# Layer 3's expert weights: from one DMA per part to one load and VectorE copies into a ring

## The chip, the cores and the metric

One NeuronCore of a Trainium2 chip runs the whole program; nothing is split over cores. The metric is the device time of one execution in microseconds. The kernel before takes 620.84 us, the median of 3 runs (620.84 to 621.14).

## The reference

Four layers run one after the other on x of 4 x 256 x 256 (1024 tokens of 256 channels). In each layer a bidirectional decay recurrence over the tokens gives weights by which sigmoid(x) is multiplied, and a mixture-of-experts FFN of that product is added to x:

```
x = x + L0_ffn(L0_cond(x, ...), ...)   # 48 kept experts, top 8, capacity 96
x = x + L1_ffn(L1_cond(x, ...), ...)   # 8 experts of 176, top 2, and a shared one
x = x + L2_ffn(L2_cond(x, ...), ...)   # 14 experts of 176, top 2, and a shared one
x = x + L3_ffn(L3_cond(x, ...), ...)   # 16 experts of 128, top 2, weights unpacked from integers
```

The change is in layer 3's FFN, where per token t and expert e:

```
logits = log_sigmoid(x @ gate_weight.T); probs = softmax(logits); topw, topi = top_k(probs, 2)
w_up, w_down = (q - 8) * blocks_scale * global_scale        # 16 x 256 x 128, 16 x 128 x 256
a = square(relu(x @ w_up[e]));  y = sum over e of (a * wdense[t, e]) @ w_down[e]
```

## The kernel before, in words

The engines run their own instruction streams and meet at semaphores. For layers 1 to 3 the 2048 pairs of a token and its expert are sorted by expert into blocks of 128 rows. In layer 3 a block has two parts of 64 rows, each with an expert of its own, since few tokens go to each of 16 experts: 24 blocks (`BK[3]`), 48 parts. The two parts are two column tiles of TensorE. VectorE computes in `block_experts` (L1306) a table `be`, which says for every part which expert it belongs to.

What happens to block b of layer 3:

- GpSimd (POOL) gathers its 128 token rows from `ctab` in DRAM into one of six buffers `xs` (`gather2`, L1682), about five blocks ahead.
- TensorE transposes them (`block_turn`, L707), ScalarE moves them to `xT_s` (`block_move`, L924), TensorE multiplies with the up weights of the two parts (`block_up`, L733, 8 matmuls), ScalarE takes the relu (`block_act`, L932), VectorE squares it (`block_hidden`, L1346), TensorE transposes that (`turn_h`, L748), ScalarE moves it (`move_h`, L939), TensorE multiplies with the down weights (`block_down`, L765, 4 matmuls), ScalarE moves the result to `o_s`, one of three buffers (`block_out`, L946), and POOL scatters it to `ybuf` in DRAM (`scatter2`, L1689).

The order of the instructions is written out by hand. TensorE's loop (L845) is, in iteration b: turn block b+2, up of block b+1, transpose of the hidden of block b, down of block b-1. POOL's loop is gather b+5, scatter b-1, and VectorE's has `block_hidden(b)` alone in layer 3.

The weights: layers 1 and 2 unpack the 16 experts of layer 3 beside their own work and store them in DRAM (`w3`: per expert 128 rows of 512 numbers, 256 up columns and 256 down columns, 256 KB). `load_parts` (L417) on SyncE's (SP's) queue then copies for every part its expert from `w3` to one of 16 places `w3r` in `wR`: a register is loaded from `be` (L425) and a DMA issued with it (L426); TensorE waits for each place (L729), and from part 16 on a DMA waits until the down product of an old part is done. `wR` holds layer 2's up weights until that layer's last block.

After the blocks SP reads `ybuf` back into `ysb` in two DMAs of 1 MB (L473), ScalarE and VectorE weigh the two rows of each token (L954, L1352), TensorE turns them back (`final`, L781), VectorE adds them to x (L1216), and x is stored.

Of the kernel before, what the change touches and what calls it, by code (L numbers as in the profile page):

```python
# [5 lines left out]
P = 128  # L6
# [43 lines left out]
NG = P // GROUP  # L50
SHW = [P, P, SH1 - 2 * P]
NSH, SHEAD = 6, 3
XB, OB, WB = 6, 3, 16

RW = 2 * KT * E2 * I2
UP1 = RW - 2 * KT * E1 * I1
assert E1 * 2 * C <= UP1 and WB * 2 * C <= RW
BM, GM = max(BK), max(k * n for k, n in zip(NP, BK))  # L60
RL = [0, UNITS, 2 * UNITS, E2 * 2]
assert RL[3] >= 3 * UNITS
# [39 lines left out]
def build(nc, xT, fT, cond, wu, o2n_row, o2n_col, gwT, rconst, gscale, wglu, wq, s_up, s_down, sel3,  # L102
          ident, tri, iota, out):
    with ExitStack() as ctx:
# [3 lines left out]
        def sem(name):  # L108
            return ctx.enter_context(nc.semaphore(name))
# [95 lines left out]
        with ExitStack() as tables:  # L205
            def sbt(name, shape, dt=F32):
# [28 lines left out]
        half_t = sb("half_t", [P, BM])  # L235
        idx_g = sb("idx_g", [P, BM], I32)
        idx_s = sb("idx_s", [P, BM], I32)
        sb("rest", [P, 2 * TT * P])
        wR = sb("wR", [P, RW])
        wU = [None, wR[:, UP1:RW].rearrange("p (q n) -> p q n", q=2 * KT),  # L240
              wR[:, :].rearrange("p (q n) -> p q n", q=2 * KT)]
        wD = [None, wR[0:IH, 0:E1 * 2 * C],
              R[0:IH, 0:E2 * 2, :].rearrange("p a n -> p (a n)")]
        w3r = wR[:, 0:WB * 2 * C].rearrange("p (w n) -> p w n", w=WB)
        w3 = nc.dram_tensor("w3", (E3, P, 2 * C), F32, kind="Internal").ap()
        ybuf = nc.dram_tensor("ybuf", (2 * TOK + BM * P, C), F32, kind="Internal").ap()
        ctab = nc.dram_tensor("ctab", (TOK, C), F32, kind="Internal").ap()
# [20 lines left out]
        shg_done, shu_done, sha_ready, shh_ready, shd_done = (  # L268
            sem("shg_done"), sem("shu_done"), sem("sha_ready"), sem("shh_ready"), sem("shd_done"))
        xs_in = [sem(f"xs_in{i}") for i in range(XB)]  # L270
        w_in = [sem(f"w_in{i}") for i in range(WB)]
        y_out = [sem(f"y_out{i}") for i in range(OB)]
        xs_turned, xs_ready, bu_done, ba_ready, bh_ready, bd_done, o_ready = (
            sem("xs_turned"), sem("xs_ready"), sem("bu_done"), sem("ba_ready"), sem("bh_ready"),
# [59 lines left out]
        def _(sp):  # L334
# [79 lines left out]
                sp.dma_start(wU[2][:, :, n * P:E2 * I2], up_of(sum(CH[:2]) + n, 0, E2 * I2 % P)  # L414
                             ).then_inc(up_in, 16)

            def load_parts():  # L417
                sp.wait_ge(be_ready, 3)
                for s in range(2):
                    sp.wait_ge(w3_in[s], 16 * E3 // 2)  # L420
                for t in range(NP[3] * BK[3]):
                    w = t % WB
                    if t >= WB:
                        sp.wait_ge(bd_done, B0[3] + (t - WB) // NP[3] + 1)
                    e = sp.value_load(be[0:1, t:t + 1], min_val=0, max_val=E3 - 1)  # L425
                    sp.dma_start(w3r[:, w, :], w3[bass.ds(e, 1), :, :].rearrange("a p n -> p (a n)")  # L426
                                 ).then_inc(w_in[w], 16)

            def load_q(e):

# [22 lines left out]
            for layer in range(1, NL):  # L453
                for hf in range(2):
                    sp.wait_ge(ctok_ready, 4 * layer + 2 * hf + 2)
                    sp.dma_start(ctab.rearrange("(i p) c -> p i c", p=P)[:, of_half(hf), :],
                                 ctok2[:, of_half(hf), :]).then_inc(ctab_in, 16)
                if layer == 1:
                    load_q(0)
                    load_q(1)  # L460
                if layer < 3:
                    sp.wait_ge(c_ready, 4 * layer + 4)
                    load_down(2, *((0, NDE), (NDE, E2))[layer - 1])
                    for e in range(DQ[layer - 1], DQ[layer - 1] + DQ[layer]):
                        store_w3(e)
                        if e + 2 < E3:
                            load_q(e + 2)
                else:
                    load_parts()
                for w in range(OB):  # L470
                    sp.wait_ge(y_out[w], 16 * len(range(w, B0[layer] + BK[layer], OB)))
                for hf in range(2):
                    sp.dma_start(ysb[:, of_half(hf), :],  # L473
                                 ybuf[0:2 * TOK, :].rearrange("(i p j) c -> p i (j c)", p=P, j=2)[:, of_half(hf), :]
                                 ).then_inc(y_in[hf], 16)
                if layer == 1:
                    load_shared(2)
                    load_up2()
            for n, (hf, m) in enumerate(BLOCKS):
                sp.wait_ge(x_ready, (NL - 1) * len(BLOCKS) + n + 1)  # L480
                sp.dma_start(out[m, :, hf * HALF:(hf + 1) * HALF], blk(x, hf, m)).then_inc(out_done, 16)
# [4 lines left out]
        def _(pe):  # L486
# [224 lines left out]
            def block_up(layer, b, e):  # L711
                n = B0[layer] + b
                s = n % 2
                pe.wait_ge(xs_ready, n + 1)
                wait(pe, bh_ready, n - 1)
                if layer < 3:
                    if b == 0:
                        pe.wait_ge(up_in, 16 * (2 * KT if layer == 1 else 4 * KT + 1))
                        pe.wait_ge(down_in[layer], 16 * (2 * KT if layer == 1 else 2))
                    if b < 2:  # L720
                        pe.wait_ge(shh_ready, NSH * (layer - 1) + SHEAD)
                    cols = wU[layer][:, :, bass.ds(e * I1, I1)].rearrange("p (q k) n -> p k q n", k=KT)
                    for kt in range(KT):
                        mm = pe.matmul(bank2(n)[:, 0:2 * I1].rearrange("p (q n) -> p q n", q=2), xT_s[:, s, kt, :],  # L724
                                       cols[:, kt, :, :], start=kt == 0, stop=kt == KT - 1, skip_group_check=True)
                else:
                    t = NP[3] * b
                    for g in range(NP[3]):
                        pe.wait_ge(w_in[(t + g) % WB], 16 * ((t + g) // WB + 1))  # L729
                    for kt in range(KT):  # L730
                        for g in range(NP[3]):
                            part = slice(g * GS[3], (g + 1) * GS[3])
                            mm = pe.matmul(bank2(n)[part, 0:P], xT_s[:, s, kt, part],  # L733
                                           w3r[:, (t + g) % WB, kt * P:(kt + 1) * P],
                                           start=kt == 0, stop=kt == KT - 1, skip_group_check=True)
                mm.then_inc(bu_done, 1)

# [13 lines left out]
            def block_down(layer, b, e):  # L751
# [5 lines left out]
                if layer < 3:  # L757
                    own = wD[layer][:, bass.ds(e * 2 * C, 2 * C)]
                    for h in range(2):
                        mm = pe.matmul(dst, hT_s[0:IH, s, h, :], own[:, h * C:(h + 1) * C], start=h == 0, stop=h == 1,  # L760
                                       skip_group_check=True)
                else:
                    for g in range(NP[3]):
                        part = slice(g * GS[3], (g + 1) * GS[3])
                        mm = pe.matmul(dst[part, :], hT_s[:, s, 0, part], w3r[:, (NP[3] * b + g) % WB, C:2 * C],  # L765
                                       start=True, stop=True, skip_group_check=True)
                mm.then_inc(bd_done, 1)

# [301 lines left out]
        def _(dve):  # L1070
# [277 lines left out]
            def weigh_second(layer, i):  # L1348
                dve.wait_ge(y0w_ready, TT * (layer - 1) + i + 1)
                if i == 0:  # L1350
                    dve.wait_ge(gk_ready, layer)
                dve.scalar_tensor_tensor(out=ysb[:, i, 0:C], in0=ysb[:, i, C:2 * C], scalar=gk[:, 1, i:i + 1],  # L1352
                                         in1=ysb[:, i, 0:C], op0=ALU.mult, op1=ALU.add).then_inc(yw_ready, 1)

            def unpack(e):
                s = e % 2
                dve.wait_ge(q_in[s], 16 * (2 + KT) * (e // 2 + 1))
# [212 lines left out]
            for layer in range(1, NL):  # L1570
# [10 lines left out]
                    shared_product(layer, 2)  # L1581
                if layer == 1:
                    dve.wait_ge(euk_ready, 1 + NL)
                for b in range(BK[layer]):
                    block_hidden(layer, b)
                    if layer < 3 and b < 4 * (QN[layer] - 1):
                        wkv_part(Q0[layer] + b // 4, b % 4)
                    e = unpacked(layer, b)
# [205 lines left out]
```

## Time and profile before

| | |
|---|---|
| median of 3 runs | 620.84 us (620.84 to 621.14) |
| the profiled execution | 620.28 us, its span 618.5 us |
| TensorE's mean granted clock | 0.873 of 2.4 GHz |
| TensorE busy | 490.7 us (79%) |
| VectorE busy | 415.4 us (67%) |
| POOL busy | 302.3 us (49%) |
| layer 3's blocks, from `be` to the last scatter | 529 to 601 us of the span |

All times in the rows below are microseconds from the start of the span, of the one profiled execution; durations in ns where they say ns. "[1.50 <-ACT a_s L932]" means that the engine sat idle for 1.50 us before the instruction and that ScalarE's instruction of line 932 ended this. A granted clock of 0.5 is 1.2 GHz, of 1.0 is 2.4 GHz. An instruction of the sequencer (a register load, a wait) has a q behind the engine's name.

### The profile page before, as it was taken

The numbers are of one execution on the slowest core, as the hardware profiler recorded it, in microseconds if no ns is written. First come the engines' busy times: TensorE is split into PE (matmuls) and PEld (weight loads), VectorE is DVE, ScalarE is ACT, GpSimd is POOL, SyncE is SP. The second block draws the span as 40 slices with busy tenths as digits, with TensorE's granted clock in tenths as the row PEclk, the third lists the DMA queues.
The fourth block names the chain that finished last, engine by engine and source line by source line (L and its number), as shares of the span: only waits on it lengthen the run. The fifth ranks groups of instructions, "written<-read, shape, count | busy, mean of one in ns | idle before, by whom it ended". The sixth has DMA issues, their size and how long they took to land.

```text
span 618.5 us, 8996 instructions
## 1 busy us (share of the span) xinstructions
PE 490.7 (79%) x2758; PEld 332.5 (54%) x2758; DVE 415.4 (67%) x803; ACT 213.9 (35%) x543; POOL 302.3 (49%) x262
## 2 busy tenths in 40 slices
PE   1867622889999999889999997899999992378863
PEld 1554421667878786645665474356676471234423
DVE  6998996599999999638786477478751568211003
ACT  2310040323222223315656243155554241145442
POOL 4106922779999941044774200347676100457750
PEclk9968755799999999699999985999999975588886
DMA  8400010599955510364676559447333401689935
GB/s 229 94 4 32 0 35 18 147 252 244 256 168 146 162 36 1 119 161 137 215 227 212 181 171 320 112 119 226 123 98 94 162 2 68 202 275 324 305 121 203
DMA packets 84927, 92.78 MB, mean 150 GB/s; under 512 B 8370, under 2 KB 64274, under 8 KB 84882
## 3 DMA queue, kind: packets, MB, share of 16 engines
q1 hardware_dynamic: 75858, 67.56, 36.7%
q0 software_dynamic: 9024, 24.65, 13.5%
q8 instruction: 24, 0.39, 0.3%
q14 instruction: 21, 0.17, 0.1%
HBM read 72.79 MB, written 19.40 MB: 149 GB/s over the span
## 4 chain that ended last, share of the span: by engine, by line
PE 56%; DVE 14%; POOL 10%; issue 8%; DMA 8%; ACT 2%; SPq 1%; DVEq 0%; POOLq 0%; ACTq 0%
PE y_ps L630 10%; PE g_ps L760 7%; PE u_ps L603 5%; PE u_ps L724 5%; PE g_ps L724 4%; POOL R L1643 4%; DMA xs<-ctab,idx_g 4%; PE y_ps L694 3%; PE g_ps L685 3%; PE y_ps L521 3%; PE r_ps L707 3%; POOL ybuf L1689 3%; PE g_ps L618 3%; PE u_ps L676 2%; PE r_ps L745 2%
## 5 line engine op out<-in xcount | busy, mean ns | idle before, releaser
L1682 POOL DMA_INDIRECT xs<-ctab,idx_g x76 | 75.9, 999 | 145.2 <-DVE idx_g L1322 114.8
L1689 POOL DMA_INDIRECT ybuf<-o_s,idx_s x76 | 77.4, 1019 | 66.2 <-ACT o_s L946 56.9
L1650 POOL DMA_INDIRECT xg<-ctab,idx x36 | 54.2, 1504 | 30.0 <-DVE idx L1463 22.5
L630 PE MATMUL y_ps<-P,o_hi 128*128 128x512 f32 x144 | 59.9, 416 | 0.2 <-DVE o_lo L1484 0.2
L630 PE MATMUL y_ps<-P,o_lo 128*128 128x512 f32 x144 | 56.6, 393 | 0.0
L707 PE MATMUL r_ps<-ident_s,xs 128*128 128x128 f32 x152 | 33.6, 305 | 19.5 <-DMA xs<-ctab,idx_g 13.7
L1346 DVE TENSOR_TENSOR h_s<-a_s 128x128 f32<-128x128 f32 x24 | 7.0, 292 | 59.7 <-ACT a_s L932 44.5
L946 ACT ACTIVATE o_s<-g_ps 128x256 f32<-128x256 f32 x76 | 29.1, 383 | 42.9 <-PE g_ps L760 30.2
L924 ACT ACTIVATE xT_s<-r_ps 128x256 f32<-128x256 f32 x76 | 28.9, 380 | 42.4 <-PE r_ps L707 41.5
L707 PEld LDWEIGHTS r_ps<-ident_s,xs 128*128 128x128 f32 x152 | 18.6, 149 | 42.4 <-DMA xs<-ctab,idx_g 21.4
L603 PE MATMUL u_ps<-xT_g,wup 128*96 128x96 f32 x384 | 37.8, 253 | 0.5 <-DVE hT L1478 0.5
L603 PEld LDWEIGHTS u_ps<-xT_g,wup 128*96 128x96 f32 x384 | 36.4, 170 | 1.1 <-DVE hT L1478 0.9
L724 PE MATMUL u_ps<-wR,xT_s 128*128 x104 | 36.2, 471 | 0.2 <-issue 0.2
L724 PE MATMUL g_ps<-wR,xT_s 128*128 x104 | 35.7, 466 | 0.0
L1096 DVE RECIPROCAL fwd<-fwd 128x256 f32<-128x256 f32 x20 | 35.1, 1753 | 0.7
L977 ACT ACTIVATE xT_g<-r_ps 128x256 f32<-128x256 f32 x36 | 13.7, 381 | 59.0 <-PE r_ps L588 58.9
L630 PEld LDWEIGHTS y_ps<-P,o_hi 128*128 128x128 f32 x144 | 27.1, 188 | 10.0 <-issue 4.5
L760 PE MATMUL g_ps<-R,hT_s 88*128 x116 | 30.6, 386 | 1.1 <-ACT o_s L946 0.7
L1471 DVE TENSOR_SCALAR P<-iota_tok,tokf 128x1024 fp32r<-128x1024 f32 x36 | 30.3, 841 | 0.4
L630 PEld LDWEIGHTS y_ps<-P,o_lo 128*128 128x128 f32 x144 | 27.1, 188 | 4.8
L939 ACT ACTIVATE hT_s<-r_ps 88x256 f32<-88x256 f32 (+1 forms) x76 | 26.3, 347 | 4.7 <-PE r_ps L745 4.1
L1643 POOL TENSOR_SCALAR R<-fs,wus 128x1024 f32<-128x1024 f32 x6 | 27.6, 4606 | 0.5
(255 smaller groups left out, 1103.2 us busy)
## 6 DMA issues: line engine op xcount, KB each, us to landing
wR<-w SPq DMA_DIRECT2D x48, 256.0 KB, 4.0
wup<-in_wglu SPq DMA_DIRECT2D x36, 256.0 KB, 3.9
ysb<-ybuf SPq DMA_DIRECT2D x6, 1024.0 KB, 6.8
wR<-in_wglu SPq DMA_DIRECT2D x4, 1216.0 KB, 10.3
wdn<-in_wglu SPq DMA_DIRECT2D x12, 384.0 KB, 4.9
raw_q<-in_wq SPq DMA_DIRECT2D x16, 256.0 KB
w<-w3o SPq DMA_DIRECT2D x16, 256.0 KB, 2.4
ctab<-ysb SPq DMA_DIRECT2D x6, 512.0 KB, 3.1
```

The source lines that it names most:

```text
L603: mm = pe.matmul(bank[:, e, q, :], wup[:, s, q * KT + kt, ee * I0:(ee + 1) * I0], xT_g[:, s, kt, ee, :], start=kt == 0, stop=kt == KT - 1, ...
L630: mm = pe.matmul(y_ps[:, m, hf, :], o[:, b, m * P:(m + 1) * P], P1[:, b, hf * HALF:(hf + 1) * HALF], start=first and n == 0, stop=last and ...
L707: mm = pe.transpose(r_ps[:, kt * P:(kt + 1) * P], xs[:, n % XB, kt * P:(kt + 1) * P], ident_s[:, :])
L724: mm = pe.matmul(bank2(n)[:, 0:2 * I1].rearrange("p (q n) -> p q n", q=2), xT_s[:, s, kt, :], cols[:, kt, :, :], start=kt == 0, stop=kt == ...
L760: mm = pe.matmul(dst, hT_s[0:IH, s, h, :], own[:, h * C:(h + 1) * C], start=h == 0, stop=h == 1, skip_group_check=True)
L946: act.activation(o_s[:, n % OB, :], g_ps[:, 1, n % 2 * C:(n % 2 + 1) * C], ACT.Copy).then_inc(o_ready, 1)
L1096: dve.reciprocal(den, den).then_inc(R_ready, 1)
L1471: dve.tensor_scalar(P1[:, b, :], iota_tok[:, :], tokf[:, j:j + 1], None, ALU.is_equal).then_inc(P1_ready, 1)
L1643: ins = pool.tensor_scalar(R[:, q:q + NB, :], fs[:, kt * NB:(kt + 1) * NB, :], wus[:, layer, 1, kt:kt + 1], 30.0, ALU.add, ALU.min)
L1650: pool.indirect_dma_start(out=xg[:, j % XG, :], out_offset=None, in_=ctab, in_offset=bass.IndirectOffsetOnAxis(ap=idx[:, j:j + 1], axis=0) ...
L1682: pool.indirect_dma_start(out=xs[:, n % XB, :], out_offset=None, in_=ctab, in_offset=bass.IndirectOffsetOnAxis(ap=idx_g[:, b:b + 1], axis= ...
L1689: pool.indirect_dma_start(out=ybuf, out_offset=bass.IndirectOffsetOnAxis(ap=idx_s[:, b:b + 1], axis=0), in_=o_s[:, n % OB, :], in_offset=N ...
```

## The change

`load_parts` is gone. `load_w3` on SP's queue loads all 16 experts once into `wR` (four DMAs of 1 MB), behind layer 2's reads of `ybuf`, as soon as layer 2's last down product is done. VectorE copies the two parts' weights of a block from there to one of three places of a new tensor `ring` (six parts); which expert is read is a register that VectorE loads from `be`. Blocks 0 and 1 are copied before VectorE's loop, block b+2 behind `block_hidden(b)`; from block 3 on the copy waits for the down product of the block that used the place before. TensorE reads `ring` in place of `w3r` and waits for one semaphore per block; its matmuls and column tiles are the same.

```diff
-XB, OB, WB = 6, 3, 16
+XB, OB, RB = 6, 3, 3
-        sb("rest", [P, 2 * TT * P])
+        ring = sb("ring", [P, RB * NP[3], 2 * C])
-        w3r = wR[:, 0:WB * 2 * C].rearrange("p (w n) -> p w n", w=WB)
+        w3r = wR[:, 0:E3 * 2 * C].rearrange("p (e n) -> p e n", e=E3)
@@ SP
-            def load_parts():
-                sp.wait_ge(be_ready, 3)
+            def load_w3():
+                sp.wait_ge(bd_done, B0[3])
                 for s in range(2):
                     sp.wait_ge(w3_in[s], 16 * E3 // 2)
-                for t in range(NP[3] * BK[3]):
-                    w = t % WB
-                    if t >= WB:
-                        sp.wait_ge(bd_done, B0[3] + (t - WB) // NP[3] + 1)
-                    e = sp.value_load(be[0:1, t:t + 1], min_val=0, max_val=E3 - 1)
-                    sp.dma_start(w3r[:, w, :], w3[bass.ds(e, 1), :, :].rearrange("a p n -> p (a n)")
-                                 ).then_inc(w_in[w], 16)
+                for e in range(0, E3, 4):
+                    sp.dma_start(w3r[:, e:e + 4, :], w3[e:e + 4, :, :].rearrange("e p n -> p e n")
+                                 ).then_inc(part_in, 16)
...
-                else:
-                    load_parts()
...
+                if layer == 2:
+                    load_w3()
@@ TensorE
-                    t = NP[3] * b
-                    for g in range(NP[3]):
-                        pe.wait_ge(w_in[(t + g) % WB], 16 * ((t + g) // WB + 1))
+                    pe.wait_ge(ring_ready, b + 1)
...
-                                           w3r[:, (t + g) % WB, kt * P:(kt + 1) * P],
+                                           ring[:, NP[3] * (b % RB) + g, kt * P:(kt + 1) * P],
...
-                        mm = pe.matmul(dst[part, :], hT_s[:, s, 0, part], w3r[:, (NP[3] * b + g) % WB, C:2 * C],
+                        mm = pe.matmul(dst[part, :], hT_s[:, s, 0, part], ring[:, NP[3] * (b % RB) + g, C:2 * C],
@@ VectorE
+            def copy_parts(b):
+                if b == 0:
+                    dve.wait_ge(be_ready, 3)
+                    dve.wait_ge(part_in, 16 * E3 // 4)
+                if b >= RB:
+                    dve.wait_ge(bd_done, B0[3] + b - RB + 1)
+                for g in range(NP[3]):
+                    t = NP[3] * b + g
+                    e = dve.value_load(be[0:1, t:t + 1], min_val=0, max_val=E3 - 1)
+                    ins = dve.tensor_copy(ring[:, NP[3] * (b % RB) + g, :],
+                                          w3r[:, bass.ds(e, 1), :].rearrange("p a n -> p (a n)"))
+                ins.then_inc(ring_ready, 1)
...
+                if layer == 3:
+                    for b in range(RB - 1):
+                        copy_parts(b)
                 for b in range(BK[layer]):
                     block_hidden(layer, b)
+                    if layer == 3 and b + RB - 1 < BK[3]:
+                        copy_parts(b + RB - 1)
```

## Rows read from the trace of the kernel before

**Rows 1.** The page, groups of instructions (part 5) and DMA issues (part 6).

```profile
L1682 POOL DMA_INDIRECT xs<-ctab,idx_g x76 | 75.9, 999 | 145.2 <-DVE idx_g L1322 114.8
L1689 POOL DMA_INDIRECT ybuf<-o_s,idx_s x76 | 77.4, 1019 | 66.2 <-ACT o_s L946 56.9
...
wR<-w SPq DMA_DIRECT2D x48, 256.0 KB, 4.0
```

**Rows 2.** Timeline, scatters of layer 3: the 3rd and the 18th.

```profile
550.26 0.99 POOL L1689 DMA_INDIRECT ybuf<-o_s,idx_s  x1 [0.30 <-issue]
...
589.30 0.99 POOL L1689 DMA_INDIRECT ybuf<-o_s,idx_s  x1 [0.38 <-ACT o_s L946]
```

**Rows 3.** Timeline, layer 3's beginning.

```profile
529.07 0.19 DVE L1312 TENSOR_SCALAR be<-bef 128x48 int32<-128x48 f32 x1
...
531.51 0.66 PE L707 MATMUL r_ps<-ident_s,xs 128*128 128x128 f32 x2 [0.52 <-issue]
...
535.04 1.12 PE L733 MATMUL u_ps<-wR,xT_s 128*64 128x128 f32 x8 [2.87 <-DMA wR<-w]
```

**Rows 4.** Timeline, one iteration of TensorE's loop at a granted clock of 1.0.

```profile
562.88 0.66 PE L733 MATMUL u_ps<-wR,xT_s 128*64 128x128 f32 x8
...
563.73 0.65 PE L765 MATMUL g_ps<-wR,hT_s 128*64 128x256 f32 x4
...
564.31 0.44 PE L707 MATMUL r_ps<-ident_s,xs 128*128 128x128 f32 x2
564.43 0.38 ACT L946 ACTIVATE o_s<-g_ps 128x256 f32<-128x256 f32 x1 [0.32 <-PE g_ps L765]
```

**Rows 5.** Timeline, up and end of down at a granted clock of 0.5.

```profile
540.49 1.12 PE L733 MATMUL u_ps<-wR,xT_s 128*64 128x128 f32 x8
...
543.11 0.38 ACT L946 ACTIVATE o_s<-g_ps 128x256 f32<-128x256 f32 x1 [0.78 <-PE g_ps L765]
```

**Rows 6.** Register loads by line: duration ns min/median/max, first and last start us.

```profile
L425 SPq TENSOR_LOAD <-be x48: 262/270/795, 529.3 to 586.0; - x48
...
L774 PEldq TENSOR_LOAD <-be x52: 297/308/830, 274.2 to 475.2; - x52
```

**Rows 7.** The same view of 530.5 to 531.8 us: the second part's load and DMA.

```profile
L425 SPq TENSOR_LOAD <-be x1: 282/282/282, 530.7 to 530.7; - x1
...
L426 SPq DMA_DIRECT2D wR<-w x2: 360/368/375, 530.3 to 531.4; - x2
```

**Rows 8.** The same view of line 89: one sequencer instruction on two engines.

```profile
L89 ACTq EVENT_SEMAPHORE  x384: 17/17/17, 119.6 to 599.2; - x192
...
L89 DVEq EVENT_SEMAPHORE  x41: 21/21/7685, 130.0 to 494.4; - x41
```

**Rows 9.** VectorE's groups by form: busy us, mean ns | idle before.

```profile
L1093 DVE TENSOR_SCALAR fwd<-fwd 128x256 f32<-128x256 f32 x12 | 13.8, 1146 | 0.0
...
L1376 DVE TENSOR_TENSOR fwd<-fwd,bwd 128x512 f32<-128x512 f32 x12 | 8.2, 684 | 0.0
...
L1378 DVE TENSOR_SCALAR fwd<-fwd 128x256 f32<-128x256 f32 x12 | 3.5, 294 | 0.4
...
L1111 DVE TENSOR_SCALAR ek<-fs 128x1024 f32<-128x1024 f32 x1 | 0.7, 682 | 0.0
```

**Rows 10.** Windows: stretch and length, busy us (instructions), then granted clock, DMA, GB/s.

```profile
530.30:543.60 13.30, 8.32 (x40) 4.33 (x40) 0.88 (x3) 3.30 (x10) 3.78 (x4) 0.50 0.83 252
...
561.60:575.30 13.70, 10.36 (x83) 5.28 (x82) 1.75 (x6) 7.33 (x23) 10.34 (x12) 1.00 0.97 315
```

**Rows 11.** Timeline, the down product of block 21.

```profile
595.43 0.65 PE L765 MATMUL g_ps<-wR,hT_s 128*64 128x256 f32 x4
```

**Rows 12.** Timeline of SP's queue behind layer 2; landing of all reads of `ybuf`.

```profile
485.43 0.93 SPq L473 DMA_DIRECT2D ysb<-ybuf  x2
...
511.31 3.02 SPq L456 DMA_DIRECT2D ctab<-ysb  x2
...
DMA to landing us min/median/max: 5.5/6.8/8.0
```

More of the change, by code:

```diff
@@ L52 @@
 NSH, SHEAD = 6, 3
-XB, OB, WB = 6, 3, 16
+XB, OB, RB = 6, 3, 3
 RW = 2 * KT * E2 * I2
 UP1 = RW - 2 * KT * E1 * I1
-assert E1 * 2 * C <= UP1 and WB * 2 * C <= RW
+assert E1 * 2 * C <= UP1 and E3 * 2 * C <= RW
 BM, GM = max(BK), max(k * n for k, n in zip(NP, BK))
@@ L270, in build @@
         xs_in = [sem(f"xs_in{i}") for i in range(XB)]
-        w_in = [sem(f"w_in{i}") for i in range(WB)]
+        part_in, ring_ready = sem("part_in"), sem("ring_ready")
         y_out = [sem(f"y_out{i}") for i in range(OB)]
```

## The prediction, made before the changed kernel was run

> **What bounds the kernel now.** I read the page's groups and DMA issues first, then the timeline of layer 3's blocks, then the register instructions by line. The change touches only the stretch between `be` (529 us) and the last scatter. There POOL sets the pace. Each block costs it a gather of 0.97 us, a scatter of 0.99 us and two pauses of 0.30 us [rows 1, 2]; from the 3rd scatter at 550.26 to the 18th at 589.30 are 15 blocks, 39.04 / 15 = 2.60 us each [rows 2]. TensorE needs less at full clock: its iteration is turn, up, transpose, down, and from the start of one up product at 562.88 to the end of the next turn at 564.75 are 1.87 us [rows 4]. It catches up at the end. The 48 weight DMAs [rows 1] hold it up once: the first up product starts at 535.04 after 2.87 us of waiting for `wR<-w`, though the second block was turned by 532.17 [rows 3]. So the DMAs that the change removes cost some 3 us at the beginning; behind it they are paced by free places and are 16 parts ahead, and no row has TensorE waiting for them after the second block.
>
> **The load of `w3`, moved.** Four DMAs of 1 MB go into SP's queue behind the two reads of `ybuf` at 485.43, and the next thing in that queue is the store of `ctab` at 511.31 [rows 12]. The two reads, of 1 MB each, land 5.5 and 8.0 us after the issue at their extremes [rows 12], so a further MB takes about 2.5 us, four take 10, and they are in by about 505. The store isn't held up, and `be`, the other condition of the copies, comes only at 529.26. Cost 0, hidden beside layer 2's end and layer 3's router. If the four did not queue behind the reads but shared with them, the second read would land up to 2.5 us later, and layer 2's end with it: bounds 0 and +2.5 us; I take 0.
>
> **The beginning of the stage.** A part costs VectorE a register load, the arithmetic on it and a copy. On SP's queue from the start of the load to the DMA that uses the register are 0.7 us (530.7 to 531.4) [rows 7], the load itself 0.27, on TensorE's queue 0.31, at the most 0.8 [rows 6]. VectorE's sequencer has no such row; its wait instruction takes 21 ns where ScalarE's takes 17 [rows 8], so I scale by 1.24 and take 0.85 us. Bounds 0.3 (a load alone) and 1.25 (0.8 for the load and SP's remaining 0.43). The copy of 128x512 f32 has no row either: the one-input forms of this engine take 294 ns at 256 and 682 at 1024 columns [rows 9], by a straight line 423 ns at 512; the two-input form takes 684 at 512, and one form of 256 columns took 1146 in the stretch where POOL computed too. I take 0.42, with bounds 0.42 and 1.15. One part's load can run while the copy before it does, not faster.
> So blocks 0 and 1 are in the ring at 529.3 + 2 x 0.85 + 0.42 = 531.4 and 533.1. The first up product starts when block 1 is turned, 532.2, instead of 535.04; block 1's follows at about 533.9, block 2's at 536.1 (its copy has no place to wait for), and the down product of block 0 ends at about 538.7, where it ended at 543.1 [rows 5]. Gain 4.4 us, at least the 2.8 of the first wait.
>
> **The ring, where the time goes.** Follow `copy_parts(b + 2)`: it waits until the down product of block b-1 is done, for that block has the place. TensorE does this down product as the last thing of iteration b, and the first thing that it needs after the next turn is up of block b+2, which waits for just that copy. Nothing of the copy can lie beside anything but the turn. In the register's path it is worse: the wait stands ahead of both register loads in VectorE's program, so none of them can run early. The cycle is therefore: down ends; 2 loads and 1 copy behind them, 0.85 + 0.85 + 0.42 = 2.12 (the first copy lies under the second load); hand over to TensorE, 0.05; up, transpose, down. Up's start to the moment at which ScalarE has the down product is 564.43 - 562.88 = 1.55 us at full clock [rows 4] and 543.11 - 540.49 = 2.62 at half [rows 5]. The square of block b+1 queues behind the copy but lies beside up of block b+2, and costs nothing. That makes 3.72 us a block at full clock and 4.79 at half, both above POOL's 2.60. Bounds: 2.74 us (full clock, loads 0.3, the two copies one behind the other: 1.55 + 0.05 + 0.30 + 0.84) and 6.3 (half clock, loads 1.25, the last copy 1.15).
> Which clock? At half clock TensorE would be busy about 3.1 of 4.79 us (the 2.62, and some 0.5 of the turn that doesn't overlap), 65%. In the beginning of this stage it was busy 8.32 of 13.30 us, 63%, and the clock stayed at 0.50; between 561.6 and 575.3 it was busy 76% and kept 1.00 [rows 10]. At full clock the cycle would leave it busy 1.8 of 3.72, 48%. So the lower level holds; since the busy part is one piece of 3 us, I grant 2 of the cycles the higher level.
> The cycle runs 21 times, from the down product of block 0 to that of block 21 (block 23 is the last one copied): 19 x 4.79 + 2 x 3.72 = 98.5 us. Down of block 21 then ends at 538.7 + 98.5 = 637.2, where it ended at 595.43 + 0.65 = 596.1 [rows 11]. Behind it nothing is changed: POOL now has no backlog, which saves a few tenths in the last scatters, and TensorE's last two blocks at the lower clock take them back.
>
> **The sum.** 637.2 - 596.1 = +41.1 us on the profiled execution's 620.28 (span 618.5 and 1.8 around it): 661.4. The median of the runs shown is 0.6 above that execution: 662.
>
> The fewer weight DMAs leave the gathers more room; TensorE waited for gathers in several places of this stage. This is worth nothing now, since each gather is issued some five blocks ahead and a block takes longer.
>
> **A rule that speaks against the change.** Rows first: POOL's gathers and scatters average 999 and 1019 ns over three layers [rows 1] against 0.97 and 0.99 in layer 3, where VectorE is nearly idle, and a one-input VectorE operation of 256 columns took 294 ns alone and 1146 beside POOL's arithmetic [rows 9]. The Trainium skill, "SBUF — State Buffer", section "SBUF: two separate sides", says that a VectorE fp32 copy from SBUF to SBUF takes a port pair that it shares with GpSimd as an exclusive lock, so that GpSimd can't write the descriptors of its DMAs meanwhile. No row of layer 3 shows it, as no such copy is there. By it POOL's block would take up to 2 x 0.42 more, which is a rival below; the sum above stays, as POOL has over 2 us to spare in the cycle.
> The skill also has a floor of about 0.6 us for a register load ("DMA: Bandwidth & Descriptors", "Latency and other measured facts"). The trace disagrees with it (0.27 and 0.31 at the median [rows 6]); by it the cycle would be some 0.6 us longer and the time about 674.
>
> **Rivals.**
> *The round trip is short* (6%): register loads of 0.3 to 0.5 us and a clock that stays up, 3.0 us a block. 538.7 + 63 = 601.7 against 596.1: 626. For it: the load alone is 0.27; against: SP's row counts 0.7 until the register is used.
> *POOL is locked out, and sets the pace* (3%): 2.60 + 0.84 = 3.44 us a block, on the 18 blocks that POOL paces, +15: 635. It decides only where the round trip is under 3.44, against which stand the loads and the clock.
> *VectorE waits for POOL instead* (5%): copies of 1.15 us. The first exceeds the load beside it by 0.30, the second by 0.73: 1.03 more in each of 21 cycles, +22: 684. For it the 1146 ns; against it that this came beside POOL's arithmetic, which layer 3 does not have.
> *The other side, faster or the same* (5%): the copy fits between down and the next up, with everything under POOL's pace. That takes a cycle of at most 2.60 us: 1.0 for both loads, copy and hand over, at full clock. Then POOL paces as before, but from 4.4 us earlier, less what its first gathers cost: 617, or nothing if POOL is slowed by as much. The lower bound of the cycle, 2.74, misses it by little; the sequencer would have to load, compute and dispatch in less than the time of a bare load.
> *The forecast* (81%): between 642 and 684 by itself.
>
> **Numbers.** 662. Left out of 640 to 686 are the short round trip, the lock on POOL and the faster case, 14%, and a few per cent of the forecast. From no change one can tell 0.2%, 1.2 us. Faster 4%, the same 1%, slower 95%.
>
> **What would show it.** Steps right: register loads on VectorE's queue that start within 0.1 us of the end of each down product; two copies per block of about 0.42 us, the second about 0.85 us behind the first; up of block b+2 waiting for VectorE (`ring`) with 1.2 to 1.7 us idle in every iteration; scatters 4.8 us apart; granted clock about 0.5 through the stage; POOL idle over 2 us a block; the first up product at about 532. Wrong: scatters still 2.6 us apart with "issue" before them; TensorE waiting for `xs` and not for VectorE; a second copy right behind the first; layer 2's end later than before, which would be the moved load. The forecast falls if a part takes under 0.5 us, or if the clock stays at 1.0.

## The result, and the profile after

| | before | after |
|---|---|---|
| median | 620.84 us (618.70 to 621.14, 4 runs) | 661.54 us (660.07 to 662.44, 4 runs) |
| ratio, 95% interval | | 1.0655 [1.0626, 1.0684] |
| the profiled execution, its span | 620.28, 618.5 us | 660.07, 658.3 us |
| TensorE's mean granted clock | 0.873 | 0.825 |

The change makes the kernel 6.5% slower; 662 was predicted. A ratio is formed from the runs within 1.5% of a kernel's fastest, which matters most for `ring3_loads_first` below, whose eleven runs spread from 622 to 641 us.

The page of the changed kernel, its parts 5 and 6 (busy us, mean ns | idle before), has the new copies, the two POOL groups of [rows 1] and the load that took the place of the 48 DMAs:

```profile
L1358 DVE COPY ring<-wR 128x512 f32 x48 | 20.5, 427 | 79.0 <-PE g_ps L759 65.6
L1694 POOL DMA_INDIRECT xs<-ctab,idx_g x76 | 77.0, 1013 | 143.5 <-DVE idx_g L1316 113.2
L1701 POOL DMA_INDIRECT ybuf<-o_s,idx_s x76 | 78.1, 1027 | 105.5 <-ACT o_s L940 98.2
...
wR<-w SPq DMA_DIRECT2D x4, 1024.0 KB, 12.9
```

The copies themselves are 20.5 us in all. What matters stands behind the bar of the first line: VectorE sat idle for 79 us in front of them, 65.6 of it for the down product (line 759). POOL's pauses in front of the scatters, which were 0.30 and 0.38 us in [rows 2], are now waits for ScalarE's `o_s`: 98.2 us in the three layers (56.9 before), 57.5 of them in layer 3.

The timeline of the changed kernel, one cycle of layer 3's blocks (start, duration, engine, line, out<-in; in brackets idle time before, and what ended it), in place of [rows 4, 5]:

```profile
558.54 1.12 PE L759 MATMUL g_ps<-ring,hT_s 128*64 128x256 f32 x4
559.59 0.69 PE L703 MATMUL r_ps<-ident_s,xs 128*128 128x128 f32 x2
559.71 0.39 ACT L940 ACTIVATE o_s<-g_ps 128x256 f32<-128x256 f32 x1 [0.79 <-PE g_ps L759]
...
560.44 0.43 DVE L1358 COPY ring<-wR 128x512 f32 x1 [3.31 <-PE g_ps L759]
...
561.18 0.43 DVE L1358 COPY ring<-wR 128x512 f32 x1 [0.31 <-issue]
...
561.76 1.12 PE L727 MATMUL u_ps<-ring,xT_s 128*64 128x128 f32 x8 [1.48 <-DVE ring L1358]
...
563.22 1.12 PE L759 MATMUL g_ps<-ring,hT_s 128*64 128x256 f32 x4
...
564.39 0.38 ACT L940 ACTIVATE o_s<-g_ps 128x256 f32<-128x256 f32 x1 [0.79 <-PE g_ps L759]
```

Read it as a circle: the down product ends (559.66), the second copy ends 1.95 us later (561.61), up starts at 561.76, the next down product ends at 564.34. From one `o_s` to the next are 564.39 - 559.71 = 4.68 us; over the whole stretch the mean is 4.65 (97.74 us for 21). TensorE sits idle for 1.48 us of this one, for `ring`; its waits of this kind are 32.5 us in all, 21 of them.

Between the end of the down product and the first copy lie the register instructions. The view by line of 1357 and 1358, VectorE's sequencer (count: duration ns min/median/max, first and last start), in place of [rows 6]:

```profile
L1357 DVEq TENSOR_LOAD <-be x48: 298/300/559, 527.6 to 630.9; - x48
...
L1357 DVEq FUSED_REGOPS  x48: 190/190/216, 528.2 to 631.2; - x48
...
L1357 DVEq SEQ_ASSERT  x48: 23/23/35, 528.4 to 631.5; - x48
...
L1358 DVEq FUSED_REGOPS  x48: 57/57/65, 528.5 to 631.5; - x48
```

And TensorE's clock. Windows of the changed kernel (stretch and length, busy us and instructions of TensorE, its weight loads, VectorE, ScalarE, POOL, then granted clock, DMA share, GB/s):

```profile
537.40:540.80 3.40, 1.87 (x17) 0.98 (x15) 1.05 (x3) 1.12 (x5) 2.09 (x2) 1.00 0.11 39
...
540.80:634.00 93.20, 62.23 (x296) 29.81 (x296) 21.36 (x61) 25.93 (x79) 35.84 (x36) 0.50 0.18 53
```

Every cycle but the first ran at the lower of the two levels, 1.2 GHz, where before the stage climbed to 1.00 [rows 10].

### The profile page after: what moved, and what is told of

Same layout as the page of the kernel before. It is cut to its first block, busy times and chain, and to the rows that moved or that the text cites. A ratio compares the mean times of both kernels' runs of the same rounds, so it can differ in the third digit from the quotient of the medians.

```text
span 658.3 us, 8927 instructions
## 1 busy us (share of the span) xinstructions
PE 513.3 (78%) x2758; PEld 339.4 (52%) x2758; DVE 433.5 (66%) x851; ACT 215.4 (33%) x543; POOL 304.5 (46%) x262
## 4 chain that ended last, share of the span: by engine, by line
PE 55%; DVE 15%; POOL 10%; issue 8%; DMA 6%; DVEq 3%; ACT 2%; SPq 0%; POOLq 0%; ACTq 0%
PE g_ps L754 7%; PE y_ps L626 6%; PE u_ps L720 5%; PE g_ps L720 5%; POOL R L1655 4%; PE g_ps L759 4%; PE y_ps L690 3%; PE u_ps L599 3%; DMA xg<-ctab,idx 3%; PE g_ps L681 3%; PE y_ps L517 3%; PE r_ps L703 2%; POOL xg L1662 2%; DVE ring L1358 2%; DVEq L1357 2%
## 5 line engine op out<-in xcount | busy, mean ns | idle before, releaser
L1701 POOL DMA_INDIRECT ybuf<-o_s,idx_s x76 | 78.1, 1027 | 105.5 <-ACT o_s L940 98.2
L1358 DVE COPY ring<-wR 128x512 f32 x48 | 20.5, 427 | 79.0 <-PE g_ps L759 65.6
L703 PE MATMUL r_ps<-ident_s,xs 128*128 128x128 f32 x152 | 36.8, 330 | 9.2 <-DMA xs<-ctab,idx_g 5.1
```

The lines of the kernel that those rows point to most:

```text
L703: mm = pe.transpose(r_ps[:, kt * P:(kt + 1) * P], xs[:, n % XB, kt * P:(kt + 1) * P], ident_s[:, :])
L1358: ins = dve.tensor_copy(ring[:, NP[3] * (b % RB) + g, :], w3r[:, bass.ds(e, 1), :].rearrange("p a n -> p (a n)"))
L1701: pool.indirect_dma_start(out=ybuf, out_offset=bass.IndirectOffsetOnAxis(ap=idx_s[:, b:b + 1], axis=0), in_=o_s[:, n % OB, :], in_offset=N ...
```

## The experiments

Theory A: the loss is the round trip through the place in the ring (down product, two register loads in a row, copies, up product), lengthened by half clock, which the idle time of the round trip itself brings about. It has two rivals: the copies or their register loads cost what they cost wherever they stand (VectorE's work is the price); or the copies disturb POOL, which sets the pace. In the expectations the times of the stretch are counted on the profiled execution. The kernel before ran again beside each group of runs: 620.96, 621.78 and 621.01 us; each ratio below is against its own neighbours.

**Is it the place that the copy waits for?** `ring4_ahead2`: a ring of four blocks (parts 6 and 7 lie in an unused end of `wR`), copies still two blocks ahead. The copy of block b+2 then waits for the down product of block b-2, and the up product that needs the copy comes a whole iteration after that, not right behind it. Everything else is the change's: 48 copies, 48 register loads, the same order.

```diff
-XB, OB, RB = 6, 3, 3
+XB, OB, RB, RA = 6, 3, 4, 2
...
+        more = wR[:, E3 * 2 * C:E3 * 2 * C + 2 * 2 * C].rearrange("p (w n) -> p w n", w=2)
+        def place(i, a, b):
+            return ring[:, i, a:b] if i < 6 else more[:, i - 6, a:b]
...
-                    if layer == 3 and b + RB - 1 < BK[3]:
-                        copy_parts(b + RB - 1)
+                    if layer == 3 and b + RA < BK[3]:
+                        copy_parts(b + RA)
```

> Ring of four blocks (eight parts; the last two lie in the unused end of wR), copied two blocks ahead as in the changed kernel. The copy of block b+2 now waits for the down product of block b-2, which was done an iteration earlier. Theory A (the reuse of the place is the round trip that costs all): no copy waits on a fresh down product, the pace is POOL's 2.6 us again from an earlier start, 612 to 619 us, faster than before. Theory B (the 48 copies themselves, or their lock against POOL's DMAs, cost the time): the same 48 copies run, so 635 us or more. Theory C (register loads on VectorE are the cost): the same loads run, so still well over 630.

Measured: 615.94 us, ratio 0.9918 [0.9874, 0.9961]; the whole loss is gone, and the kernel is slightly faster than the one before. The timeline of this kernel, the 3rd scatter, two with the copies beside them, and the 18th:

```profile
547.63 0.99 POOL L1706 DMA_INDIRECT ybuf<-o_s,idx_s  x1 [0.30 <-issue]
...
563.56 0.43 DVE L1363 COPY ring<-wR 128x512 f32 x1 [0.33 <-issue]
...
563.75 1.10 POOL L1706 DMA_INDIRECT ybuf<-o_s,idx_s  x1 [0.30 <-issue]
...
566.47 0.99 POOL L1706 DMA_INDIRECT ybuf<-o_s,idx_s  x1 [0.30 <-issue]
...
566.84 0.43 DVE L1363 COPY ring<-wR 128x512 f32 x1 [1.52 <-PE g_ps L764]
...
587.73 0.99 POOL L1706 DMA_INDIRECT ybuf<-o_s,idx_s  x1 [0.30 <-issue]
```

Scatters are (587.73 - 547.63) / 15 = 2.67 us apart and begin after "issue" again: POOL paces the stage, as in [rows 2] with 2.60. And what TensorE waits for between 540 and 590 us (us in all, times, longest) is the gathers' data; for `ring` it waits once, for 0.3 us. Some copies still wait for a down product, but with an iteration to spare:

```profile
PEld r_ps L708 <- DMA xs<-ctab,idx_g: 13.9, 12, 2.0
DVE ring L1363 <- PE g_ps L764: 10.1, 8, 1.5
...
PE g_ps L732 <- DVE ring L1363: 0.3, 1, 0.3
```

So the price is neither the copies nor the loads as such. What is left of them is the 0.07 us by which POOL's block is longer (some scatters 1.10 for 0.99). The profiled execution takes 55.21 us from the first `o_s` to that of block 21, where the kernel before takes 53.02; the gain lies in the earlier beginning, 9.73 us from `be` to the first `o_s` for 14.04.

**Does looking further ahead help?** `ring4_ahead3`: the same ring, but copies three ahead (`RA = 3`), so that a copy waits for the down product of block b-1 again, while its data are needed an iteration later.

> Ring of four blocks, copied three blocks ahead: the copy of block b+3 stands behind the square of block b and waits for the down product of block b-1, as in the changed kernel, but up of block b+3 needs it only two iterations later. Theory A in its bare form (only TensorE's wait for the ring counts): back to POOL's pace, 612 to 619 us. Theory A with VectorE's order (the square of block b+1 queues behind a copy that waits): cycle = wait, two loads and two copies 1.95, square 0.3, transpose and down 1.5 at half clock or 0.9 at full, so 3.1 to 3.8 us a block, 630 to 645 us.

Measured: 638.06 us, 1.0258 [1.0185, 1.0332], a cycle of 3.73 us. The bare form of A (only up of the copied block can be late) is wrong here; the other order counts. VectorE is one queue: the square `h_s` of block b+1 stands behind copies that wait. The timeline of this kernel:

```profile
562.48 0.43 DVE L1363 COPY wR<-wR 128x512 f32 x1 [2.35 <-PE g_ps L764]
...
563.43 0.28 ACT L931 ACTIVATE a_s<-u_ps 128x128 f32<-128x128 f32 x1 [0.68 <-PE u_ps L732]
563.56 0.28 DVE L1345 TENSOR_TENSOR h_s<-a_s 128x128 f32<-128x128 f32 x1
...
563.90 0.47 PE L747 MATMUL r_ps<-ident_s,h_s 128*128 128x128 f32 x1 [0.52 <-DVE h_s L1345]
```

Up runs early now (562.26), but the transpose of the hidden waits for VectorE, and the clock is at 0.50 throughout. So here a wait does harm through what is queued behind it, and not through its own data alone.

**How much of the cycle are the register loads?** `ring3_loads_first`: the change with its ring of three, the two loads of a block put ahead of the wait for the place.

```diff
+                own = [dve.value_load(be[0:1, t:t + 1], min_val=0, max_val=E3 - 1)
+                       for t in range(NP[3] * b, NP[3] * (b + 1))]
                 if b >= RB:
                     dve.wait_ge(bd_done, B0[3] + b - RB + 1)
-                for g in range(NP[3]):
-                    t = NP[3] * b + g
-                    e = dve.value_load(be[0:1, t:t + 1], min_val=0, max_val=E3 - 1)
+                for g, e in enumerate(own):
```

> The changed kernel with both register loads of a block ahead of the wait for the down product; ring of three blocks. Theory A: the chain from down to up shrinks from 1.95 to about 0.95 us (two copies back to back), the cycle from 4.67 to 3.7 us at half clock, 21 cycles, 640 us; where the clock rises (TensorE then busy 85 per cent) down to 625. If the loads did not lie on the chain: no change, 661.

Measured: 635.46 us, the median of eleven runs. Four lie between 622.34 and 628.49, and the ratio, 1.0054 [1.0001, 1.0106], holds for these; seven lie between 632.52 and 640.71. The profiled execution is one of the seven (639.43) and is read here only for its cycle at half clock, which the change has too (windows, then timeline):

```profile
541.00:620.00 79.00, 66.35 (x309) 30.95 (x307) 19.78 (x61) 27.47 (x83) 39.70 (x39) 0.50 0.23 66
```

```profile
570.63 0.38 ACT L940 ACTIVATE o_s<-g_ps 128x256 f32<-128x256 f32 x1 [0.79 <-PE g_ps L759]
570.74 0.77 DVE L1358 COPY ring<-wR 128x512 f32 x2 [2.69 <-PE g_ps L759]
...
571.65 1.12 PE L727 MATMUL u_ps<-ring,xT_s 128*64 128x128 f32 x8 [0.45 <-ACT xT_s L918]
...
574.28 0.38 ACT L940 ACTIVATE o_s<-g_ps 128x256 f32<-128x256 f32 x1 [0.79 <-PE g_ps L759]
```

Both copies come in one piece right behind the down product, and the cycle is 3.65 us where the change has 4.67: the loads' place in the path costs 1.02 us a cycle, with the clock at 0.50 in both. Up now waits for `xT_s`, that is for the turn at half clock, and no longer for the copies.

**How much is the clock?** `ring3_filler` and `ring3_filler5`: the change with nine, then five, useless 128x128 f32 matmuls on TensorE between turn and up of each iteration, in the gap in which it waits for `ring`. Their result is thrown away.

```diff
+                    if layer == 3 and 1 < b + 1 < BK[layer]:
+                        for _ in range(5):
+                            pe.matmul(y_ps[:, 0, 0, 0:P], ident_s[:, :], ident_s[:, :], start=True, stop=True,
+                                      skip_group_check=True)
```

> The changed kernel, with nine matmuls of 128x128 f32 of no use between the turn and the up product of each iteration, into a bank that layer 3's blocks don't use; they fill TensorE's wait for the ring. If the half clock is a consequence of that wait and adds 1.1 us to each cycle: the clock is about 1.0 in the stage, the cycle 3.5 to 3.7 us, 636 to 642 us. If the clock stays low whatever fills the gap: the filler takes 2.0 us of the 1.5 free, 0.5 more in each of 21 cycles, 672 us.

> As the kernel with nine matmuls between turn and up, but with five. Nine took 2.17 us where only 1.5 were free, and so made the cycle 3.81 us themselves. Five take 1.1 us. If the half clock comes from TensorE's wait: clock 1.0 in the stage (it was with nine), cycle 1.95 (wait, loads, copies) + 1.55 (up to down at full clock) = 3.5 us, 21 cycles x 1.17 less than the changed kernel's 661.5: 637 us. If five don't hold the clock up: 655 to 662.

Measured: nine matmuls 646.03 us, 1.0383 [1.0309, 1.0457]; five 639.64, 1.0284 [1.0229, 1.034]. I had sized the nine by half: a matmul is two instructions of 0.12 us in the records, 18 of them take 2.17 us and themselves set the cycle (3.81 us). Five fit. Windows of the two kernels, nine and then five:

```profile
541.00:620.00 79.00, 77.98 (x670) 60.85 (x672) 21.40 (x61) 26.49 (x84) 37.01 (x38) 1.00 0.21 63
```

```profile
541.00:620.00 79.00, 63.09 (x525) 44.45 (x523) 22.24 (x64) 27.05 (x85) 40.22 (x41) 1.00 0.23 67
```

The granted clock is 1.00 in both, where the change had 0.50. The cycle with five, from its timeline:

```profile
562.15 0.38 ACT L944 ACTIVATE o_s<-g_ps 128x256 f32<-128x256 f32 x1 [0.32 <-PE g_ps L759]
...
562.31 1.28 PE L845 MATMUL y_ps<-ident_s 128*128 128x128 f32 x10
...
564.19 0.66 PE L727 MATMUL g_ps<-ring,xT_s 128*64 128x128 f32 x8 [0.60 <-DVE ring L1362]
...
565.74 0.38 ACT L944 ACTIVATE o_s<-g_ps 128x256 f32<-128x256 f32 x1 [0.32 <-PE g_ps L759]
```

565.74 - 562.15 = 3.59 us: half clock costs the change 4.67 - 3.59 = 1.08 us a cycle, some 22 us or half of its loss, and TensorE still waits for `ring`.

**Do the two terms add up?** `ring3_loads_first_filler3`: both edits at once, with three matmuls, since the gap is smaller.

> The ring of three with both terms taken off it at once: register loads ahead of the wait, and three useless matmuls (0.24 us each at half clock, 0.12 at full) between turn and up. Theory A says that a cycle of the change is 4.67 us = 2.57 for the bare round trip (two copies, up, transpose, down, hand over) + 1.02 for the loads + 1.08 for the half clock. If the terms add up, the cycle is 2.6 to 2.9 us (a few tenths where the three matmuls, 0.4 us, stand in the way), against POOL's own pace of 2.6 to 2.7: 21 x 2.75 = 58 us from the first o_s to that of block 21, against 97.7, so 660.1 - 40 = 620, range 617 to 626, with a granted clock of 1.0 through the stage. Rival: the terms overlap (the loads' place on the path is taken by something else, the clock gives its time back only where the wait is long): cycle of 3.1 us or more, 630 and above. If three matmuls are too few the clock falls again and the time is that of the loads alone, 635 to 640.

Measured: 617.41 us, 0.9962 [0.9933, 0.9991]. The ring of three, at no loss at all. Timeline and windows of this kernel:

```profile
569.09 0.38 ACT L944 ACTIVATE o_s<-g_ps 128x256 f32<-128x256 f32 x1 [0.31 <-PE g_ps L759]
...
569.21 0.93 DVE L1362 COPY ring<-wR 128x512 f32 x2 [1.60 <-PE g_ps L759]
569.25 0.83 PE L845 MATMUL y_ps<-ident_s 128*128 128x128 f32 x6
...
569.84 1.14 POOL L1698 DMA_INDIRECT xs<-ctab,idx_g  x1 [0.30 <-issue]
...
573.98 0.99 POOL L1705 DMA_INDIRECT ybuf<-o_s,idx_s  x1 [0.30 <-issue]
...
574.63 0.56 DVE L1362 COPY ring<-wR 128x512 f32 x1 [1.61 <-PE g_ps L759]
```

```profile
541.00:593.00 52.00, 49.04 (x407) 32.45 (x402) 20.76 (x58) 24.51 (x77) 37.58 (x36) 1.00 0.31 93
```

The three matmuls (six instructions) take 0.83 us, twice the 0.4 of the expectation, and still fit. The stretch of 21 cycles takes 56.15 us (536.97 to 593.12), 2.67 each; most are 2.69. The terms predict 4.67 - 1.02 - 1.08 = 2.57. Between `ring3_filler5` and this kernel, both at a granted clock of 1.00, the loads' place is worth 3.59 - 2.69 = 0.90 us.

Two loops now have the same length: the round trip (0.16 us from the end of down to the copies, 0.89 for the two, 0.14, and 1.5 from up to the end of down), and POOL's (1.09 for the gather at the median, 0.99 for the scatter, 2 x 0.30). They also touch. The first copy of a pair begins 0.66 us into a scatter (574.63 and 573.98) and takes 0.555 us at the median for 0.427; it ends 0.23 us after the scatter. That is about the 0.12 us by which the cycle is longer than the terms say. The gather then begins while the second copy runs, and takes 1.09 for 0.97. The rows don't tell which of the two loops leads.

**Do the copies disturb POOL, and does the kind of instruction matter?** `ring4_two_inputs`: `ring4_ahead2` with the copy done as a maximum of the tensor with itself, a two-input instruction (684 ns at 512 columns in [rows 9], 693 here). The edit changes the kind of the instruction and its length at once.

```diff
-                    ins = dve.tensor_copy(place(NP[3] * (b % RB) + g, 0, 2 * C),
-                                          w3r[:, bass.ds(e, 1), :].rearrange("p a n -> p (a n)"))
+                    own = w3r[:, bass.ds(e, 1), :].rearrange("p a n -> p (a n)")
+                    ins = dve.tensor_tensor(place(NP[3] * (b % RB) + g, 0, 2 * C), own, own, ALU.max)
```

> Ring of four blocks, copied two ahead, but each copy is a tensor_tensor with the same tensor as both inputs (maximum) in place of a tensor_copy: 684 ns by the rows of before, in place of 427. In the ring of four with plain copies POOL's scatters took 1.02 to 1.18 us beside the copies, against 0.99 in the kernel before, and its pace was 2.67 us a block, not 2.60. If that is the one-input copy holding a port that POOL's DMA instructions need for writing: durations back to 0.97 and 0.99, pace 2.60, 1.2 us less than with plain copies (614 to 616). If any VectorE work on SBUF does it, or the longer work does: durations the same or longer, pace 2.67 or more, 615 to 618.

Measured: 619.71 us, 0.9981 [0.9948, 1.0015], against 0.9918 [0.9874, 0.9961] with the copy; the intervals just overlap, so the times alone only suggest that it is slower. That two-input instructions leave POOL alone was wrong. The timeline of this kernel, POOL and the instruction in the copy's place:

```profile
564.17 1.44 DVE L1364 TENSOR_TENSOR ring<-wR 128x512 f32 x2 [0.59 <-issue]
565.08 1.39 POOL L1706 DMA_INDIRECT ybuf<-o_s,idx_s  x1 [0.30 <-issue]
566.68 0.69 DVE L1364 TENSOR_TENSOR wR<-wR 128x512 f32 x1 [0.86 <-PE g_ps L764]
566.78 1.44 POOL L1699 DMA_INDIRECT xs<-ctab,idx_g  x1 [0.30 <-issue]
```

Most gathers and scatters keep their 0.97 and 0.99; about one in five takes 1.2 to 1.5 us, where the longest beside the one-input copy took 1.18. Between 540 and 590 us the gathers average 1101 ns here, 1001 in `ring4_ahead2` and 970 before.

The start times say when this happens. The scatter at 565.08 began while VectorE's instruction ran that ended at 565.61, and ended 0.86 us after it (566.47). In `ring4_ahead2` the scatter at 563.75 began under the copy that ended at 563.99 and ended, again, 0.86 us after it (564.85), while the scatter at 566.47 began before the copy of 566.84 and kept its 0.99. In these two kernels, all 30 gathers and scatters that began at least 0.06 us into such an instruction and 0.15 us before its end ended 0.82 to 0.87 us after it; those that began while none ran took 0.95 to 1.03 us. So what counts is how much of VectorE's instruction is left when POOL's begins. The two-input one does more harm because it is longer; no difference by its kind is seen.

**Can the ring of four do better?** At the beginning of the stage its TensorE still ran at half clock. `ring4_warm`: `ring4_ahead2` with eight and then five useless 128x512 f32 matmuls on TensorE, while it has nothing to do before and behind the sorting of layer 3's tokens. `ring4_warm_filler`: this, and three fillers per iteration.

```diff
+            def warm(n):
+                for _ in range(n):
+                    pe.matmul(y_ps[:, 0, 0, :], ident_s[:, :], x[:, 0, 0:HALF], start=True, stop=True,
+                              skip_group_check=True)
...
+                if layer == 3:
+                    warm(8)
                 lists2(layer)
+                if layer == 3:
+                    warm(5)
```

> Ring of four, copied two ahead, and matmuls of no use while TensorE waits in layer 3's router: eight of 128x512 f32 before the list products, five behind them, so that the blocks don't start at half clock. With half clock the down product of block 0 was done 9.7 us after the table of experts, of which 6.5 would be left at full clock; POOL's pace starts from there: 612 to 613.5 us, 2.5 to 3.5 less than the ring of four alone. If the clock can't be raised there, or POOL's first gathers set the start: 615 to 617, and 618 if the fillers delay the lists.

> The kernel with warm-up matmuls, and three matmuls of 128x128 f32 more between turn and up of every iteration (0.65 us at full clock), so that TensorE's clock stays up inside the stage. The ring of four had it at 0.5 for a third of the stage. If POOL's pace of 2.67 us a block is the only bound: the same time as with warm-up alone, within 1 us. If the stretches of half clock cost in the ring of four, where TensorE needs 3.15 us a block: 1 to 3 us less. If the filler gets in the way of gathers that are late: 1 to 2 us more.

Measured: 613.61 us, 0.9863 [0.9817, 0.9909], the lowest of all, though its interval overlaps that of `ring4_ahead2` (0.9918 [0.9874, 0.9961]); the gain over it rests on the trace. With the fillers 617.94, 0.9943 [0.9912, 0.9974]. Windows of `ring4_warm`, the beginning and the middle of the stage:

```profile
521.50:548.80 27.30, 23.39 (x151) 11.54 (x149) 16.68 (x42) 9.63 (x30) 14.47 (x15) 1.00 0.22 65
548.80:590.00 41.20, 33.44 (x239) 17.04 (x239) 17.55 (x46) 20.09 (x63) 30.73 (x31) 0.88 0.34 99
```

The first `o_s` comes 7.31 us after `be`, against 9.73 in `ring4_ahead2` and 14.04 before; the 21 cycles take 52.34 us (53.02 before). With fillers the clock stays at 1.00 but the 21 cycles take 54.37: most are 2.47 us long, where `ring4_warm` has cycles of 1.80; the fillers stand in front of ups that could run. From `be` to the reads of `ybuf` behind the blocks the loss is 2.7 us. The profiled execution was another 6.5 us late at `be` already. The fillers stand in layer 3 only; what the traces show ahead of it is a granted clock of 0.51 from 132 to 139 us and from 350.5 to 354, where `ring4_warm` had 1.00, and 4.6 of the 6.5 us had come about by 156 us. Why the clock fell there is open.

## Why the prediction was right

**The moved load, cost 0: right.** It was issued at 486.38 and its four pieces were in at 504.5 (I had said 505), the reads of `ybuf` ahead of it landed at 491.23 and 493.88 as before (491.24, 493.88), and the store of `ctab` wasn't late. The timeline of SP's queue, in place of [rows 12]:

```profile
486.38 6.87 SPq L422 DMA_DIRECT2D wR<-w  x4
...
509.60 3.02 SPq L452 DMA_DIRECT2D ctab<-ysb  x2
```

**The beginning, gain 4.4: right, 4.3 measured.** The rows that answer to [rows 3]:

```profile
527.35 0.19 DVE L1306 TENSOR_SCALAR be<-bef 128x48 int32<-128x48 f32 x1
...
530.20 1.12 PE L727 MATMUL u_ps<-ring,xT_s 128*64 128x128 f32 x8
```

From `be` to the first up are 2.85 us for 5.97, and to the first `o_s` 9.72 for 14.04.

**The price of a part: right within its bounds, a little high.** 0.74 us from load to copy for the 0.85 taken (300 + 190 + 23 + 57 ns, and some 0.17 between them), the copy 427 ns for 423. The scaling from SP's queue was the better of the two bounds; the bare load of 0.30 would have missed by more. The load shows no floor of 0.6 us here either, so that the Trainium skill's figure ("DMA: Bandwidth & Descriptors", "Latency and other measured facts") is contradicted by a third queue.

**The round trip that can't hide: right, and it is the whole loss.** Cycle 4.67 us for 4.79 at half clock: 1.95 for 2.12 from the end of down to that of the second copy, 0.15 for 0.05 of handing over, 2.58 for 2.62 from up to the end of down. `ring4_ahead2` takes the wait off the path and keeps all copies and loads: the loss goes.

**The clock: right in kind, wrong in the mix.** I had granted two cycles the higher level; one got it (3.59 us), twenty ran at half clock, 18 of them in 4.67 us and two in 5.03. The errors cancel nearly: 19 cycles 0.12 us too long in the forecast (-2.3), one at the wrong level (+0.95), two longer by 0.36 (+0.7), the one at full clock 0.13 shorter: 97.7 for 98.5. Also `ring3_filler5` measures what half clock costs, 1.08 us a cycle, where the prediction had 4.79 - 3.72 = 1.07. Its argument by busy time, however, does not carry far: `ring3_loads_first` was busy for 66.35 of 79.00 us and stayed at 0.50 in the profiled execution, `ring4_ahead3` for 58.77 of 69.00, and the kernel before itself had a stretch of 6.80 us (554.8 to 561.6), busy for 5.67, at 0.50. That the lower level came was right, but not by this argument.

**The end, nothing: off by 1.1.** From the `o_s` of block 21 to the end are 23.46 us for 22.34: the last blocks and the first of the final turns still ran at half clock, more than POOL's empty backlog gave back.

**The sum.** Measured: -1.7 (`be` came at 527.35 for 529.07, since the half-clock stretch of TensorE began 3 us later in the router; this distance differs between runs of kernels that are equal up to there) - 4.3 + (97.74 - 53.02) + 1.1 = +39.8, the difference of the spans. Predicted: +41.1. That the median came within 0.5 us of the 662 is in part luck: beside the errors of the clock, which cancel, the profiled execution gained 1.7 us ahead of the stage, and it lies 1.5 us under the median of its runs, where 0.6 was taken.

**The rivals.** The short round trip needed register loads of 0.3 to 0.5 us until the register is used, and full clock, and got neither (0.74 us a part, 0.50); `ring3_loads_first_filler3` takes both loads out of the way, has the full clock, and lands at 617, where the rival "faster or the same" had put it: the circle has come down to POOL's pace. POOL locked out: there is a trace of it, far below the 0.84 us a block of that rival. In `ring4_ahead2` POOL's block is 0.07 longer, single instructions 0.99 to 1.18. The rule of the Trainium skill ("SBUF — State Buffer", "SBUF: two separate sides") says that the shared port pair goes to whichever instruction starts first, for the whole of it, and beside the copy it names VectorE instructions with two SBUF inputs, against a GpSimd instruction that reads SBUF. The traces agree for both kinds: what POOL began under either ended 0.82 to 0.87 us after it, and the first copies of `ring3_loads_first_filler3` ended 0.23 us after a scatter. The rival's price was too high because the two seldom meet in that order. In the change, 6 of 44 gathers and scatters of the stage began under a copy; in nearly every cycle the scatter begins 0.07 us ahead of the copy (560.37 and 560.44) and keeps its 0.99. VectorE waiting for POOL (copies of 1.15 us): not at all in the change (427 ns), though `ring3_loads_first_filler3` has copies of 0.555. The 1146 ns behind this rival is a mean of two sorts: eight of the twelve ran beside POOL's arithmetic and took 920 to 2025 ns, the other four 275 to 289.

## What to carry to other kernels

Count a buffer that one engine fills and another empties by the round trip of a place: with n places and copies n-1 ahead, in an order like this one, the wait, the register load, the copy and the use stand one behind the other; here one more place, not one copy less, is worth 45 us of 660. Put register loads (and all else that needs no place) ahead of the wait. And before a producer's wait is put into an in-order queue, look at what stands behind it: copying further ahead made the ring of four worse, not better.

## What the runs showed of the hardware that was not expected

- Idle time and half clock went together, and filling the idle time brought full clock: the gap of 1.48 us per cycle goes with a granted clock of 0.50 over 93 us. Ten useless instructions per cycle in just this gap (1.28 us) brought 1.00 over 79 us and made the kernel 22 us faster.
- The same program can go either way: `ring3_loads_first` took between 622 and 641 us. The mean granted clock of the whole run is on record for each: 0.869 to 0.873 in the four fastest, 0.826 to 0.848 in the other seven. I have a profile only of one of the seven, at 0.50 through the stage; that the four had 1.00 there is inferred from their means and from `ring3_loads_first_filler3`, where it is at 1.00 and the time at 617.
- A GpSimd DMA instruction that begins while an f32 instruction of VectorE with 512 columns runs (past its first 0.06 us and before its last 0.15) ended 0.82 to 0.87 us after it (30 of 30, one input or two), so 0.97 or 0.99 us become up to 1.48; begun before it, it keeps its length. A copy begun 0.66 us into a scatter ended 0.23 us after it, 0.555 us long for 0.427.
- TensorE reading its weights straight from `wR` by a register's address, without any copy, was not tried; whether it would be cheaper is open.
